# Attention on one Trainium2 core: where and how often the softmax reciprocals are turned and stored

## What is computed

```python
B, S, HID = 64, 32, 512          # as called; D, HQ, HK = 128, 32, 8
q, k, v = x @ Wq.T, x @ Wk.T, x @ Wv.T    # then RMS norm and RoPE on q and k
k_all = concatenate([k_cache[block_table], k], axis=1)     # 512 cached + 32 own keys
v_all = concatenate([v_cache[block_table], v], axis=1)
scores = einsum('bqhd,bkhd->bhqk', q, k_all) * SCALE       # 4 query heads per key head
scores = where(valid, scores, -1e30)
probs = softmax(scores, axis=-1)
o = einsum('bhqk,bkhd->bqhd', probs, v_all).reshape(B, S, HQ * D)
return einsum('bse,de->bsd', o, Wo)
```

## Time and profile before

| | |
|---|---|
| time, median of 3 runs | 2466.95 us (2465.81 to 2468.25) |
| profiled execution | 2452.79 us, its span 2451.0 us |
| granted TensorE clock, mean | 0.998 |
| PE busy | 2398.8 us (98%) |
| DVE busy | 1888.7 us (77%) |
| ACT busy | 1320.1 us (54%) |
| POOL busy | 716.6 us (29%) |
| moved by DMA | 542.36 MB, mean 221 GB/s |
| attention, first to last L1227 | 819.1 to 2000.2 us |
| output projection, first to last matmul | 2003.7 to 2368.9 us |

### The profile page before, as it was taken

How to read it: one execution, slowest core, us unless ns; L and a number is a source line. 1 busy time by engine, 2 the same in 40 slices (tenths; PEclk the granted TensorE clock), 3 DMA queues, 4 the chain that set the end, 5 groups by cost and what they waited for, 6 DMA issues and landing times. The chain is left out here.

```text
span 2451.0 us, 53992 instructions
## 1 busy us (share of the span) xinstructions
PE 2398.8 (98%) x16104; PEld 2163.3 (88%) x16104; DVE 1888.7 (77%) x3317; ACT 1320.1 (54%) x3758; POOL 716.6 (29%) x712
## 2 busy tenths in 40 slices
PE   5999999999999999999999999999999999999999
PEld 4888877777778999999999999999999997777777
DVE  7559999999961888888888888888888867665653
ACT  2335555555533677777777777777777751111120
POOL 1206666666641122222222222222222211231100
PEclk9999999999999999999999999999999999999999
DMA  8732333333346688888889888888888887666522
GB/s 312 258 120 87 94 94 98 94 116 94 94 128 239 225 299 277 295 304 295 281 297 303 289 284 299 303 284 288 302 297 283 294 286 253 215 196 214 189 69 103
DMA packets 434117, 542.36 MB, mean 221 GB/s; under 512 B 36980, under 2 KB 350100, under 8 KB 429460
## 3 DMA queue, kind: packets, MB, share of 16 engines
q1 hardware_dynamic: 390724, 394.24, 48.7%
q0 software_dynamic: 36864, 134.23, 16.2%
q10 hardware_dynamic: 6480, 13.26, 1.5%
HBM read 440.59 MB, written 101.01 MB: 221 GB/s over the span
## 5 line engine op out<-in xcount | busy, mean ns | idle before, releaser
L1296 DVE CUSTOM_DVE_ANT_0 at_sm<-ps,at_mask 128x544 f32<-128x544 f32 x512 | 370.2, 723 | 234.4 <-PE ps L1209 225.8
L1242 PE MATMUL ps<-at_pt,at_v_raw 128*128 128x128 f32 x4096 | 540.9, 275 | 1.9 <-issue 1.9
L1242 PEld LDWEIGHTS ps<-at_pt,at_v_raw 128*128 128x128 f32 x4096 | 497.6, 192 | 2.1 <-issue 2.1
L1359 ACT ACTIVATE at_pt<-ps 128x512 f32<-128x512 f32 x512 | 305.7, 597 | 297.2 <-PE ps L1218 285.5
L942 POOL TENSOR_TENSOR pr_m<-pr_qn,tb 128x256 f32<-128x256 f32 x320 | 331.7, 1056 | 307.3 <-DVE pr_qn L911 292.2
L1372 ACT ACTIVATE at_pr<-at_sm,at_nm 128x544 f32<-128x544 f32 x512 | 383.6, 749 | 15.1 <-DVE at_nm L1296 11.2
L1289 DVE TENSOR_TENSOR at_k_lo<-shared,at_k_hi 128x1088 fp32r<-128x1088 f32 x256 | 325.8, 1273 | 0.0
L762 PE MATMUL ps<-pr_hi,xh 128*128 (+1 forms) x768 | 317.8, 414 | 5.8 <-DVE pr_qn L911 4.9
L1167 POOL DMA_INDIRECT at_v_raw<-v_cache,at_idx x256 | 277.0, 1082 | 113.8 <-issue 61.8
L1218 PE MATMUL ps<-constants,at_pr 128*128 128x128 f32 x2048 | 306.5, 272 | 0.0
L763 PE MATMUL ps<-pr_lo,xh 128*128 (+1 forms) x768 | 303.3, 395 | 0.0
(11 more groups left out here) (239 smaller groups left out, 4304.4 us busy)
## 6 DMA issues: line engine op xcount, KB each, us to landing
shared<-k_t SPq DMA_DIRECT2D x1024, 128.0 KB, 4.6
qk_t<-pr_stage SPq DMA_DIRECT2D x160, 256.0 KB, 2.3
shared<-qk_t SPq DMA_DIRECT2D x64, 512.0 KB, 7.8
o_t<-at_ot SPq DMA_DIRECT2D x64, 512.0 KB
shared<-ri_d SPq DMA_DIRECT2D x32, 1024.0 KB, 8.2
o_raw<-o_t SPq DMA_DIRECT2D x32, 1024.0 KB, 6.1
f_w<-wqkv SPq DMA_DIRECT2D x12, 1024.0 KB, 5.9
s_k_in<-k_cache SPq DMA_DIRECT2D x16, 512.0 KB, 7.5
```

The costliest lines, as they stand in the source:

```text
L1242: e.matmul(sums(w, k), v_raw[:, q, c, g * D:(g + 1) * D], pt[:, jj % 4, c * P:(c + 1) * P], start=(k == 0 and c == 0), stop=False, skip_gr ...
L1296: e.tensor_tensor_reduce(out=halves(sm[:, r, :]), in0=ps[:, 2 * r:2 * r + 2, 0:W], in1=halves(mask[:, q, :]), scale=-SC, scalar=3e38, op0= ...
L1359: e.activation(pt[:, jj % 4, :], ps_w(jj % 2), ACT.Copy).then_inc(s_pt, 1)
```

## The change

The reciprocals of all 64 batches stay in SBUF: `ri` becomes 128 x 512 (column b * 8 + g), and L1277 writes its four columns at an address that goes with the unit. No batch of the loop turns, copies or stores them. In the last iteration TensorE turns three blocks of 128 columns (batches 0 to 47) where batch 62's turn was, and the fourth (batches 48 to 63) where batch 63's was; ScalarE copies 128 x 384 and 128 x 128. SP stores three blocks of 128 rows x 512 bytes before the seam's loads, waits for them to land, and stores the fourth between the output stores of batches 62 and 63. In DRAM `ri_d` is now [b, g, 128], so that the reciprocals of one head and 16 batches are 16 runs of 512 bytes, 4 KB apart, where they were one run of 8 KB. The landing of the reciprocals has a semaphore with the clearing of `v_new` (`s_cleared_rs`), and `s_ot` counts 16 per batch. The diff, without the renamings:

```diff
-        self.nm, self.su, self.ri = (place(n, [P, 2 * REP]) for n in ("nm", "su", "ri"))
+        self.nm, self.su = (place(n, [P, 2 * REP]) for n in ("nm", "su"))
...
-        rt = sb("rt", [UB, 2, P])
+        ri = sb("ri", [P, B * UB])
+        rt = sb("rt", [P, CB, P])
...
-        turned = lambda w: ps[:, 6 - w, 0:2 * P]
+        all_turned = lambda w: ps[:, 6 - w, :]
+        turned = lambda w: ps[:, 6 - w, 0:P]
...
             def store(b, q):
-                e.wait_ge(s_rt, b + 1)
                 at = bass.ds(b, 1) if not isinstance(b, int) else slice(b, b + 1)
-                e.dma_start(ri_d[:, at, :].rearrange("g o x -> g (o x)"), rt[:, q, :]).then_inc(s_ot[q], 16)
                 e.wait_ge(s_o, (b + 1) * 2 + 1)
                 e.dma_start(o_t[at, :, :].rearrange("o d x -> (o d) x"), ot[:, q, :]).then_inc(s_ot[q], 16)
...
             part = o_raw.shape[2]
+
+            def store_ri(c):
+                e.dma_start(ri_d[c * part:(c + 1) * part, :, :].rearrange("b g x -> (b g) x"), rt[:, c, :]).then_inc(s_cleared_rs, 16)
+
+            e.wait_ge(s_rt, 1)
+            for c in range(CB - 1):
+                store_ri(c)
             e.wait_ge(s_lo, (B - 1) * (UB // 2))
+            e.wait_ge(s_cleared_rs, 1 + 16 * (CB - 1))
             for c in range(2):
                 for q in range(2):
-                    e.wait_ge(s_ot[q], 32 * (c + 1) * part // 2 + 32)
-                e.dma_start(ri_b[:, c, :], ri_rows(ri_d, 0, c)).then_inc(s_or[c], 16)
+                    e.wait_ge(s_ot[q], 16 * (c + 1) * part // 2 + 16)
+                e.dma_start(by_batch(ri_b[:, c, :]), ri_rows(ri_d, 0, c)).then_inc(s_or[c], 16)
                 e.dma_start(o_raw[:, c, :, :], o_t[c * part:(c + 1) * part, :, 0:P].rearrange("b d x -> d b x")).then_inc(s_or[c], 16)
                 if c == 0:
                     e.dma_start(w_raw[:, :, :], dram["wo"][0:REP, :, :].rearrange("h d o -> d h o")).then_inc(s_w, 16)
             store(B - 2, 0)
+            e.wait_ge(s_rt, 2)
+            store_ri(CB - 1)
             store(B - 1, 1)
...
                     e.wait_ge(s_o, i * 4 + n + 1)
-                    if w == 1:
+                    if isinstance(u, int) and u >= PER and w == 1:
                         e.wait_ge(s_ri, i * 4 + n + 1)
-                        e.transpose(turned(w)[0:UB, P:2 * P], ri[:, :], ident)
+                        for c in range(CB - 1) if jj < UB else range(CB - 1, CB):
+                            e.transpose(all_turned(w)[:, (1 + c % (CB - 1)) * P:(2 + c % (CB - 1)) * P], ri[:, c * P:(c + 1) * P], ident)
...
                         wait(e, s_wn, i * 4 + jj // QU)
-                        if w == 0:
-                            wait(e, s_rt, i * 2 + jj // UB)
+                        if isinstance(u, int) and u >= PER and jj == UB:
+                            e.wait_ge(s_rt, 1)
...
-                    e.reciprocal(ri[:, mine], su[:, mine]).then_inc(s_ri, 1)
+                    e.reciprocal(ri[:, of], su[:, mine]).then_inc(s_ri, 1)
...
-                    if w == 1:
-                        e.activation(rt[:, (jj // UB) % 2, :], turned(w)[0:UB, P:2 * P], ACT.Copy).then_inc(s_rt, 1)
+                    if isinstance(u, int) and u >= PER and w == 1:
+                        part = slice(0, CB - 1) if jj < UB else slice(CB - 1, CB)
+                        e.activation(rt[:, part, :].rearrange("p c x -> p (c x)"),
+                                     all_turned(w)[:, P:(1 + part.stop - part.start) * P], ACT.Copy).then_inc(s_rt, 1)
...
-    row = ri_d[bass.ds(g, 1), c * n:(c + 1) * n, :] if not isinstance(g, int) else ri_d[g:g + 1, c * n:(c + 1) * n, :]
-    return row.rearrange("o b x -> o (b x)").broadcast_to([P, n * P])
+    head = bass.ds(g, 1) if not isinstance(g, int) else slice(g, g + 1)
+    return ri_d[c * n:(c + 1) * n, head, :].rearrange("b o x -> o b x").broadcast_to([P, n, P])
...
-    ri_d = scratch("ri_d", [HK, B, P])
+    ri_d = scratch("ri_d", [B, HK, P])
```

More of the change, by code:

```diff
@@ L1013, in __init__ @@
         self.pr_new = place("pr_new", [P, 2, REP * S])
-        self.nm, self.su, self.ri = (place(n, [P, 2 * REP]) for n in ("nm", "su", "ri"))
-        place("gap", [P, 168])
+        self.nm, self.su = (place(n, [P, 2 * REP]) for n in ("nm", "su"))
+        place("gap", [P, 176])
         self.q_hi = place("q_hi", [P, 2, HK * P], F32R)
@@ L1086, in attention @@
         pt_new = sb("pt_new", [P, 2, P])
-        rt = sb("rt", [UB, 2, P])
+        ri = sb("ri", [P, B * UB])
+        rt = sb("rt", [P, CB, P])
         s_rows = sem("rows")
-        s_v, s_one, s_idx, s_mask, s_qlo, s_hi, s_lo, s_s, s_max, s_e, s_ri, s_nc, s_c, s_cn, s_pt, s_wn, s_rt, s_nw, s_o = (
-            sem(n) for n in ("v", "one", "idx", "mask", "qlo", "hi", "lo", "s", "max", "e", "ri", "nc", "c", "cn",
+        s_v, s_cleared_rs, s_idx, s_mask, s_qlo, s_hi, s_lo, s_s, s_max, s_e, s_ri, s_nc, s_c, s_cn, s_pt, s_wn, s_rt, s_nw, s_o = (
+            sem(n) for n in ("v", "cleared_rs", "idx", "mask", "qlo", "hi", "lo", "s", "max", "e", "ri", "nc", "c", "cn",
                              "pt", "wn", "rt", "nw", "o"))
```

30 lines of the change are left out of this document (18 added, 12 removed).

## The result

| | before | after |
|---|---|---|
| median of the runs | 2467.55 us (2465.81 to 2468.25, 4 runs) | 2618.32 us (2615.64 to 2625.02, 4 runs) |
| ratio, 95% interval | | 1.0617 (1.0604 to 1.0630) |
| profiled execution, span | 2451.0 us | 2617.4 us |
| mean granted clock | 0.998 | 0.974 |
| TensorE matmul, busy share | 98% | 94% |

A forecast was written before the change was run, and what follows sets the result against it. TensorE's own time was taken to bound attention and projection. 6.8 us saved, a 6.6 us stall at the turn between them, 0.1 us for the third chunk and 0.6 for the clock gave +0.5 us: 2467.5 us, range 2462 to 2473.5.

The forecast's parts named there:

- What leaves TensorE: Attention loop: batches 0 to 61 lose their turn of the reciprocals, 0.11 us each, 6.8 us saved.
- What leaves or joins engines with idle time: Attention loop: fewer ScalarE copies and SP stores, and VectorE's computed write address, change the time by nothing.
- What the change delays: Turn to the projection: SP's first loads wait behind new steps; o_raw lands at 1998.9, w_raw at 2002.3.
- later chunks have room: Projection after the third chunk: the reciprocals' loads take 1.45 us longer, which fits before VectorE even waits.
- The first load 12.4 us later: Turn to the projection: SP issues its first load at 1988.7, after the wait, three stores and their landing.
- What these are late for: End of attention: TensorE waits about 4 us, the projection starts 6.6 us late, plus 0.6 us for the clock.
- sum of +0.5 us: Whole kernel: -0.2 us from saving and stall, +0.1 us third chunk, +0.6 us clock, giving 2467.5 us.
- The rival that short runs pace the projection: Projection: reciprocal loads landing after over 11.9 us reach TensorE; at 14 us, +61 us, 2528 us; chance 3%.
- The clock rival: Turn to the projection: TensorE's clock falls in the stall and costs the whole 2.7 us, 2469.5 us; chance 20%.
- 14 us onto the median: Whole kernel: profiled 2452.79 us against median 2466.95 us; the edit's places don't depend on this, so its difference goes onto the median.

The follow-up runs named there:

- padded version: The changed kernel with a ninth, unused row behind each batch's eight rows of reciprocals in DRAM, so runs lie 4608 B apart; ratio 1.0000, again 0.9999.
- long runs: The changed kernel with reciprocals put in head order by VectorE and read as 8 KB runs again; 2452.92 us, ratio 0.9994.
- early turn: The changed kernel with rows 4608 B apart and three blocks of reciprocals turned half a batch earlier; ratio 0.9984, on another chip 0.9980.
- second `o_raw` last: The changed kernel with rows 4608 B apart, first o_raw and w_raw loads ahead of the reciprocals' stores, second o_raw load last; ratio 0.9999.

## Why the prediction was wrong, by its own steps

- **What leaves TensorE**, 62 turns of 0.11 us, 6.8 us: right. 6.9 and 7.1 to 7.5 us on two kinds of chip, in each pair of traces. The start-to-start reading of the earlier trace rows was the right price.
- **What leaves or joins engines with idle time**, nothing: right. The padded version keeps every one of these edits, its loop gains the full 6.9 us, and it is level with before.
- **What the change delays**: here is the failed step, the sentence that the new layout has "the same shape as o_raw's" and so costs 4.1 us for a MB in place of 2.65. A load of reciprocals took 22.4 to 23.0 us to land, against the 9.65 that 8.2 + 1.45 makes. o_raw's runs have the same 512 B, but its 128 partitions read rows of their own; the reciprocals' sixteen rows are the same for all, and 4096 B apart. Size and number of runs were equal and proved harmless; I priced by shape, where the addresses decided. At 768, 1024 or 4608 B the same step is right, and generous: 9.0 us. With it fell the sentence that later chunks have room, so that the loss came in 30 chunks of the projection (133.2 us) and only 16.6 us at the seam.
- **The first load 12.4 us later**: right. In the padded version it went at 1983.00, 4.8 us after the turn of the reciprocals (1978.20); in before 7.8 us ahead of it (1976.30 against 1984.11). That is 12.6 us. From this load to the landing of `o_raw` it took 10.7 us and to that of `w_raw` 13.4, where I had 10.2 and 13.6.
- **What these are late for**, a stall of 6.6 us and 0.6 for the clock: right in sum for a kernel with quick loads: with the 0.1 us I had 7.3 us at the seam, and the padded version lost 7.0 there. The shares were off (4.85 us on TensorE in one pause for my 4, and the clock of 0.73 over 6 us, 1.6 us, for my 0.6). The sum of +0.5 us stands beside a measured 1.0000. For the changed kernel itself it fell with the step above: 15.01 us of pause.
- **The rival that short runs pace the projection** had the mechanism, the rows (one set for 128 partitions, 4096 B apart) and the sign of the DMA share, and got 3%. Its threshold and price were off as well: it counted 1 us of time for each us of landing above 11.9. Two buffers stand between: two chunks take landing + 7.6 us, so the cost starts near a landing of 15.2 us and is half a us each. 13.6 us of median landing cost about 9 us in a single run, not the 49 that it would have given.
- **The clock rival** (20%) was right in kind: clocks of 0.73 and 0.76 stand behind pauses of 4.85 and 4.28 us. The length of the pause alone doesn't decide below that: behind 2.96 us (long runs) it was 0.75 and behind 2.00 us (early turn) 0.72, but behind 2.23 us (second `o_raw` last) 1.00. The page "TensorE: Matmul & The Clock Gate" of the Trainium skill, section "What's actually happening", has low speed as the default state; the traces agree where the clock fell, at 1.4 to 1.7 us for each such stretch of 6 us.
- **14 us onto the median**: right as a sum, and now with a likely cause. Before's trace is of the kind of chip where half a batch takes 9.396 us; its timed runs have times of the other kind, where the loop alone takes 11.7 us more.

## What to carry to other kernels

A load that one set of rows serves to all partitions is priced by the distance of its rows, not by the size of its runs: before a scratch tensor's axes are exchanged, write down the distance of the rows that one load reads, and pad it off 2048, 4096 and 8192 B. A landing time in a double-buffered loop costs nothing up to (period of two chunks less the steps from use to next issue), then half of what is above; work that sum out with the slowest landing that can be thought of before giving such a rival 3%. And compare one loop's pace in two traces only after knowing that the chips give the unchanged kernel the same pace.

## What the chip showed that I had not expected

- 1 MB read as the same sixteen 512-B rows by 128 partitions lands in 9.0 us at 768, 1024 and 4608 B between rows, 13.6 at 2048, 22.4 at 4096, 44.4 at 8192, and 9.0 at 512 KB; with own rows for each partition 8.9 us at 4096 B. The distance is from the start of one row to the start of the next.
- Such a load slows its neighbours: o_raw's median landing went from 6.1 to 13.3 us, an issue of `w_raw` held SP for 12.99 us, and TensorE stood 6.98 us for a value gather.
- Chips differ by 12 to 20 us in this kernel. Between two of them 11.7 us of it lie in the attention loop, and on every slower chip ScalarE has 54 to 58 waits of up to 2.5 us without a releaser between 900 and 1960 us, about one a batch, whatever the version of the kernel.
